# Logits by slots turned out of VectorE's copy behind scores 3, and the max subtraction in two halves by bank

## What is computed

```python
xn = rms_norm(x, gamma_x)
se = rms_norm(slot_embeds, gamma_slot)
logits = jnp.einsum('bsd,etd->bset', xn, se)
dispatch = jax.nn.softmax(logits, axis=1)          # over the tokens s
slots = jnp.einsum('bsd,bset->betd', xn, dispatch)
h = jax.nn.gelu(slots @ w1, approximate=False)
processed = h @ w2
combine = jax.nn.softmax(logits.reshape(b, s, e * t), axis=-1)   # over the slots
out = jnp.einsum('bnd,bsn->bsd', processed.reshape(b, e * t, d), combine)
```

## Time and profile before

| | us |
|---|---|
| median of 3 executions | 509.27 (509.1 to 510.19) |
| the profiled execution | 508.64 |
| its span, first to last instruction | 506.6 |
| TensorE busy, matmuls | 462.0 (91%) |
| VectorE busy | 376.6 (74%) |
| ScalarE busy | 312.4 (62%) |
| GpSimd busy | 175.0 (35%) |

### The profile page before, as it was taken

One profiled execution on the slowest core, in us unless ns is written; L12 is line 12 of the kernel. 1 busy time (PEld: TensorE's weight loads), 2 busy tenths in 40 slices (PEclk: granted clock), 3 DMA queues, 4 the chain that ended last, 5 costly groups with the idle time before them and its releaser, 6 DMA issues.

```text
span 506.6 us, 16039 instructions
## 1 busy us (share of the span) xinstructions
PE 462.0 (91%) x5768; PEld 377.2 (74%) x5768; DVE 376.6 (74%) x937; ACT 312.4 (62%) x544; POOL 175.0 (35%) x278
## 2 busy tenths in 40 slices
PE   3067999999999999999999999999999999999996
PEld 2046787878778787877878787787878778787875
DVE  3878696878868687887968777796877789595651
ACT  3345757566674856667575766757476675747571
POOL 4415143341515234251523425151442425144120
PEclk9559999999999999999999999999999999999999
DMA  2500203030020202011020202002020200202000
GB/s 65 122 6 9 48 12 54 5 56 8 20 45 10 52 9 53 0 30 32 10 52 10 52 0 48 14 10 52 10 52 0 56 6 10 43 12 43 12 3 10
DMA packets 45779, 14.46 MB, mean 29 GB/s; under 512 B 35640, under 2 KB 45624, under 8 KB 45752
## 3 DMA queue, kind: packets, MB, share of 16 engines
q1 hardware_dynamic: 45000, 13.80, 13.3%
q10 hardware_dynamic: 752, 0.30, 0.3%
HBM read 3.61 MB, written 2.10 MB: 11 GB/s over the span
## 4 chain that ended last, share of the span: by engine, by line
PE 74%; DVE 17%; issue 6%; ACTq 1%; ACT 1%; DVEq 0%; POOL 0%; POOLq 0%
PE x L904 14%; PE p_s L942 14%; PE x L1056 13%; PE p_s L960 9%; PE x L1029 6%; PE x L1067 6%; PE p_f L929 3%; DVE maxima L723 3%; DVE maxima L729 3%; PE x L983 2%; PE x L1037 2%; DVE arg L691 2%; PE x L1013 2%; DVE small L675 2%; DVE s_sb L697 2%
## 5 line engine op out<-in xcount | busy, mean ns | idle before, releaser
L436 POOL TENSOR_TENSOR s_sb<-s_sb,causal 128x256 f32<-128x256 f32 x128 | 94.1, 735 | 267.9 <-ACT s_sb L497 267.9
L697 DVE TENSOR_TENSOR s_sb<-p_s,causal 128x384 f32<-128x384 f32 x128 | 70.9, 554 | 62.1 <-PE p_s L942 59.7
L497 ACT ACTIVATE s_sb<-p_s 128x384 f32<-128x384 f32 x128 | 62.7, 490 | 77.2 <-PE p_s L942 77.1
L942 PEld LDWEIGHTS p_s<-feat 64*64 64x64 f32 x2048 | 78.6, 133 | 38.3 <-issue 30.2
L942 PE MATMUL p_s<-feat 64*64 64x256 f32 (+3 forms) x2048 | 100.2, 311 | 5.9 <-DVE s_sb L697 5.0
L492 ACT ACTIVATE feat<-arg,f_bias 128x512 f32<-128x512 f32 x128 | 89.7, 714 | 0.1
L691 DVE TENSOR_SCALAR arg<-p_f,f_low,f_high 128x512 f32<-128x512 f32 x64 | 51.6, 806 | 30.6 <-PE p_f L929 30.6
L1056 PE MATMUL x<-w_sb,hid_t 128*128 128x128 f32 x512 | 65.7, 281 | 0.0
L1056 PEld LDWEIGHTS x<-w_sb,hid_t 128*128 128x128 f32 x512 | 59.6, 191 | 6.6 <-issue 6.6
L960 PE MATMUL p_s<-s_sb,vw 128*32 128x128 f32 x1536 | 48.6, 274 | 5.1 <-DVE s_sb L697 5.1
L691 DVE TENSOR_SCALAR arg<-p_g,f_low,f_high 128x512 f32<-128x512 f32 x64 | 51.4, 802 | 0.0
(11 more groups left out here) (132 smaller groups left out, 835.2 us busy)
## 6 DMA issues: line engine op xcount, KB each, us to landing
xin<-in_L_attn_x_dram SPq DMA_DIRECT2D x32, 64.0 KB, 2.4
out_dram<-out_sb SPq DMA_DIRECT2D x32, 64.0 KB, 2.1
se_rows<-n_L_ffn_slot_embeds_dram SPq DMA_DIRECT2D x1, 256.0 KB, 4.5
w_f<-in_L_ffn_w_dram SPq DMA_DIRECT2D x1, 256.0 KB, 4.6
w_sb<-in_L_ffn_w_dram SPq DMA_DIRECT2D x1, 256.0 KB, 4.5
stack_t<-stack SPq DMA_TRANSPOSE x16, 4.4
bqkv_bc<-in_L_attn_bqkv_dram ACTq DMA_DIRECT2D x1, 192.0 KB, 5.0
wqkv_f<-in_L_attn_Wqkv_dram SPq DMA_DIRECT2D x1, 192.0 KB, 4.9
```

The costliest lines, as they stand in the source:

```text
L436: pool.tensor_tensor(v, v, m, ALU.mult).then_inc(mb_ok, 1)
L497: nc.scalar.activation(s_sb[:, p, 1, :], p_s[:, 1, 0:384], ACT.Copy).then_inc(eb_ok, 1)
L697: nc.vector.tensor_tensor(s_sb[:, p, 0, :], p_s[:, 0, 0:384], causal[:, :], ALU.mult).then_inc(ea_ok, 1)
L942: mm = nc.tensor.matmul(p_s[rows:rows + 64, u, o:o + hi - lo], f[:, T + keys:T + keys + 64], f[:, lo:hi], start=True, stop=True, skip_grou ...
```

## The change

The logits by slots are no longer computed by matmuls from the inputs. VectorE copies each tile of the logits by tokens out of its bank of `x01` into a new buffer `log_sb` in SBUF, and the same instruction gives the maximum of each row as its accumulator output. TensorE then transposes the eight 128 by 128 blocks of `log_sb` into `x23`.

In order: the copies with the token maxima move from stage 3 to stage 2, behind `add_attention` and ahead of `qk_norms`. The transposes stand behind scores 3, ahead of `project(b, 3)`, where the products stood ahead of scores 3. The slot maxima stay ahead of `evac_a(b, 3)`, and each half raises `mx_ok` for itself. `shift` is done in two calls, one for each half of the slots.

```diff
             def token_maxima(b):
 
-                after(dve, lg_ok, count(b, 3, 1))
-                nc.vector.tensor_reduce(maxima[:, 4:6], x01[:, :, :], AX_X, ALU.max)
+                after(dve, lt_ok, count(b, 2, 0))
+                for j in range(TILES):
+                    after(dve, lg_ok, count(b, 2, j + 1))
+                    nc.vector.tensor_scalar(log_sb[:, j, :], x01[:, j, :], 1.0, LOWEST, ALU.mult, ALU.max,
+                                            accum_out=maxima[:, 4 + j:5 + j]).then_inc(lc_ok, 1)
 
             def slot_maxima(b):
 
                 for h in range(2):
-                    after(dve, lg_ok, count(b, 3, 2 + h))
-                    last = nc.vector.tensor_reduce(maxima[:, 2 * h:2 * h + 2],
-                                                   x23[:, h, :].rearrange("p (c t) -> p c t", t=T), AX_X, ALU.max)
-                last.then_inc(mx_ok, 1)
+                    after(dve, lt_ok, count(b, 2, h + 1))
+                    nc.vector.tensor_reduce(maxima[:, 2 * h:2 * h + 2], x23[:, h, :].rearrange("p (c t) -> p c t", t=T),
+                                            AX_X, ALU.max).then_inc(mx_ok, 1)
...
-                    mm = three(x01[:, j, :], hi[:, sl], lo[:, sl], se_hi[:, :], se_lo[:, :], True, False)
-                mm.then_inc(lg_ok, 1)
-
-            def logits_slots(b):
-                hi, lo = xt_hi[:, b[1], :], xt_lo[:, b[1], :]
+                    three(x01[:, j, :], hi[:, sl], lo[:, sl], se_hi[:, :], se_lo[:, :], True, False).then_inc(lg_ok, 1)
+
+            def logits_turned(b):
+                after(pe, lc_ok, count(b, 2, 2))
                 for c in range(NCH):
                     if c % 2 == 0:
                         after(pe, (o1_ok, o2_ok)[c // 2], count(b, 1, 0))
-                    sl = slice(128 * c, 128 * c + 128)
-                    mm = three(x23[:, c // 2, T * (c % 2):T * (c % 2) + T], se_hi[:, sl], se_lo[:, sl], hi, lo,
-                               c % 2 == 0, False)
+                    for j in range(TILES):
+                        o = T * (c % 2) + 128 * j
+                        mm = nc.tensor.matmul(x23[:, c // 2, o:o + 128], log_sb[:, j, 128 * c:128 * c + 128],
+                                              ident[:, :], start=(j == 0 and c % 2 == 0), stop=False,
+                                              is_transpose=True, skip_group_check=True)
                     if c % 2 == 1:
-                        mm.then_inc(lg_ok, 1)
+                        mm.then_inc(lt_ok, 1)
...
-            def shift(b):
-
-                after(pe, mx_ok, count(b, 1, 1))
-                for c in range(NCH):
+            def shift(b, h):
+
+                after(pe, mx_ok, count(b, 2, h + 1))
+                for c in (2 * h, 2 * h + 1):
...
-                mm.then_inc(shd_ok, 1)
+                if h == 1:
+                    mm.then_inc(shd_ok, 1)
```

More of the change, by code:

```diff
@@ L28 @@
 CLIP = 20.0
+LOWEST = -3.0e38
 BLOCKS = ((0, 0, 0, T, 0), (64, 64, 64, T, 64), (128, 0, 128, 192, 256), (192, 64, 128, T, 256))
@@ L159, in build @@
         maxima = sb("maxima", [128, 6], BF16)
+        log_sb = sb("log_sb", [128, TILES, SLOTS])
         disp = sb("disp", [128, TILES, SLOTS])
@@ L251, in build @@
         lg_ok = sem("lg_ok")
+        lc_ok = sem("lc_ok")
+        lt_ok = sem("lt_ok")
         mx_ok = sem("mx_ok")
@@ L850, in row @@
                     if s == 3:
-                        token_maxima(b)
                         slot_maxima(b)
@@ L872, in row @@
                             add_attention(bp)
+                        token_maxima(b)
                         if nxt:
@@ L1015, in shift @@
                                               start=False, stop=True, skip_group_check=True)
-                mm.then_inc(shd_ok, 1)
+                if h == 1:
+                    mm.then_inc(shd_ok, 1)
                 ni = neg_ident[:, :].rearrange("p (a t) -> p a t", a=1).broadcast_to([128, 2, 128])
                 for j in range(TILES):
-                    for h in range(2):
-                        v = x23[:, h, :].rearrange("p (c t) -> p c t", c=2)[:, :, 128 * j:128 * j + 128]
-                        mm = nc.tensor.matmul(v, maxima[:, 4 + j:5 + j].broadcast_to([128, 128]), ni,
-                                              start=False, stop=True, skip_group_check=True)
-                mm.then_inc(shc_ok, 1)
+                    v = x23[:, h, :].rearrange("p (c t) -> p c t", c=2)[:, :, 128 * j:128 * j + 128]
+                    mm = nc.tensor.matmul(v, maxima[:, 4 + j:5 + j].broadcast_to([128, 128]), ni,
+                                          start=False, stop=True, skip_group_check=True)
+                if h == 1:
+                    mm.then_inc(shc_ok, 1)
             def slot_sums(b, half):
@@ L1122, in row @@
                         logits_tokens(b, nxt)
-                        logits_slots(b)
                     if s == 3:
+                        logits_turned(b)
                         project(b, 3)
-                        shift(b)
+                        shift(b, 0)
+                        shift(b, 1)
                     if s == 4:
```

## The result

The changed kernel takes 505.38 us (median of 9, 505.04 to 507.78) against 509.27 in the same comparison (median of 9): a ratio of 0.9927, 95% interval 0.9913 to 0.9941. It is 3.9 us faster, where I had forecast 7.3 us slower. Its profiled execution took 505.23, 3.4 us less than the one before.

A forecast was written before the change was run, and what follows sets the result against it. The VectorE, GpSimd, ScalarE chain was taken to bound out_sb to context, TensorE the rest. Slot maxima 0.51 us later in 14 passes (7.1), plus 0.2 for first and last, gave 516.6 us; range 512.5 to 520.5.

The forecast's parts named there:

- What bounds the kernel: From out_sb to context one chain, VectorE, GpSimd, ScalarE, with TensorE slack 0.33 us; from context on TensorE carries the pass.
- The third stretch: From context to the next out_sb: 19.85 us, TensorE busy for 19.52 of it.
- The wait for the logits and the copies: Behind out_sb on VectorE: 0.94 us waiting until the second copy starts, then that copy, 0.62 plus 0.08 for its accumulator.
- My upper bound: Dearest copy, 0.73 us plus 0.19 accumulator: slot maxima end 0.73 us later, kernel time 519.9 us.
- T: End of VectorE's slot maxima, 3.84 us behind out_sb before; forecast 0.51 later, at 4.35.
- The norms take 1.10 as before: VectorE's qk_norms, now behind the copies and ahead of the slot maxima, were to keep their 1.10 us.
- From T to `context` it takes 5.55 us: Way from the slot maxima's end through qk_newton, GpSimd and ScalarE to context: unchanged at 5.55 us.
- a longer idle time of TensorE ahead of `context`: Sign expected in the new profile: TensorE idle ahead of context for longer than the 0.33 us before.
- C: Rival: hidden room in the chain, as in qk_newton, takes up half the delay; 512 to 513.5 us; chance 0.13.
- A: Rival: TensorE's saved 0.5 us a pass counts, 501.3 us; smaller gain through sooner evac_b(b, 4), 505 to 508; together 0.07.
- The two halves of `shift`: Only the second half stays behind the slot maxima; slot_sums 0.23 us sooner, but the time doesn't change by it.
- TensorE's relief: Twelve products (1.52 us) out, eight transposes (1.00) in: 0.5 us less a pass, ahead of context, only widening a wait.

The follow-up runs named there:

- b_mask: Kernel before, with GpSimd's mask_b(b, 3) moved behind stack_low instead of ahead of qk_apply; 513.40 us against 509.27.
- b_both: Kernel before, with GpSimd's mask_b(b, 3) behind stack_low and residual and place_v behind the pass's last mask; 513.29 us.
- a_whole: Changed kernel with the max subtraction (shift) in one piece again, behind both slot maxima; 517.81 us.
- b_order: Kernel before, with only the token maximum, still a reduction of both tiles, moved ahead of qk_norms; logits by slots stay products; 524.85 us.
- b_late: Kernel before, with GpSimd's residual and place_v for the next sequence behind the pass's last mask instead of behind mask_b(b, 2); 507.19 us.
- b_mask_held: Kernel before, with GpSimd's mask_b(b, 3) behind stack_low, and stack_low made to wait for VectorE's copy stack_again; 505.70 us.
- a_whole_held: Changed kernel with the max subtraction in one piece, and GpSimd's stack_low made to wait for VectorE's copy stack_again; 506.93 us.
- b_halves: Kernel before, with only the max subtraction (shift) split in two halves by bank; 509.86 us.
- a_held_twice: Changed kernel with GpSimd's stack_low waiting for VectorE's stack_again, and project(b, 3)'s matmuls issued twice in each pass; 505.21 us.

## Why the prediction was wrong

*What bounds the kernel.* Right: the chain `out_sb`, VectorE, GpSimd, ScalarE, `context`, and TensorE from there on. The third stretch stayed at 19.84 to 19.98 in the middle passes of all variants. The way from ScalarE's end to `context` stayed at 0.10 where the copy was short; in b_mask, b_both, a_whole and b_order, where it was long, it was 0.70 to 0.88, and the transposes of the slots came last.

*The wait for the logits and the copies.* Right to 0.01: the second copy starts 1.28 behind `out_sb`. The copy's step is 0.61 to 0.62; its accumulator row lasts 0.085 and costs 0.06 behind the first copy and nothing behind the second, where I had put 0.08. So the norms start 0.09 sooner than in the sum. My upper bound had a slip that played no part: a first copy of 0.92 would have held up the second, as it has only 0.69 before that, so T would have been later by 0.96 and not 0.73.

*"The norms take 1.10 as before."* Wrong: 0.84. In the 1.10 there were 0.27 of waiting for GpSimd's residual, and the change moved the norms away from it. Of the 0.33 by which T comes sooner than forecast, this is most. b_late gets the same step back by moving the residual instead.

*"From T to `context` it takes 5.55 us", by a chain that "isn't touched".* This is the step that failed and turned the sign: 5.18, 0.37 to 0.45 less. Here too a stretch that I took over as a duration contained a wait, and what it waited for wasn't behind T but beside it: GpSimd's mask, which hangs on `evac_b(b, 3)` and not on T. So T could move by 0.18 at no cost, and since the mask ended 0.19 sooner behind `out_sb`, `context` came 0.19 sooner. I had placed `evac_b(b, 3)` behind ScalarE's logarithm and exponential, at 278.4, which is 3.59 behind `out_sb`, and asked of the mask only whether it would be done before `qk_n`. It came at 3.29, because the norms ended sooner than in my sum. An estimate from these rows: with it at 3.59 the mask would have ended at 4.94 and the first step of `qk_newton` at 5.02 instead of 4.91, a loss of 0.11 a pass and not of 0.51. b_mask_held shows what the mask held back: with it gone, `stack` comes 0.47 to 0.55 sooner behind T, and the rest of the way is TensorE's 5.23. With 0.51 expected, -0.33 on the first stretch and -0.37 on the second leave about -0.20 a pass. Of my signs, a longer idle time of TensorE ahead of `context` didn't come either: 0.19 instead of 0.33.

*The rivals.* C named the right place, "`qk_newton`, whose first step lasts 0.68 ... seems to hold a wait", and let it take back half of the 0.51; it had no price worked out, and the norms' step, 0.47 for 64 columns, had the same mark. A's time (505 to 508 for a part of it) fits the result by luck. Its mechanism was `evac_b(b, 4)` coming sooner by the halves; but `stack` behind it waited 0.51 for `qk_n`, and what came sooner was `evac_b(b, 3)`. My range ended above the result, as C's share was cut off at half of the shift.

*The two halves of `shift`.* "The time doesn't change by it" was right of the chain and wrong of the kernel: a_whole costs 12.4 us. I had walked the way to `context` on the engines' queues, and had the slack of TensorE right (5.23 against 5.18, as a_whole_held shows), but not the order of two engines at one memory. It is also where the transposes earn something: only with them does the first half start ahead of T, so that the halves bring the copy forward (3.31 behind T); in b_halves they don't (3.58 to 3.66).

*TensorE's relief.* Its 0.23 in a_held_twice was worth nothing, as forecast. But that the products no longer stand ahead of scores 3 is what let `evac_b(b, 3)` come sooner, by the rows; here I had looked at how much work was removed and not at what stood behind it.

## What to carry to other kernels

Before a duration is carried over into a sum, hold it against the same instruction elsewhere and against its size: 0.47 or 0.68 us for 64 columns is a wait, and if its end follows the end of an instruction on the other engine by a constant, it goes or comes as the two move against each other. Then measure the chain through that other instruction too. Where VectorE and GpSimd both work from SBUF, read them side by side, and let a semaphore decide who is first instead of 0.2 us of luck: one wait was worth 8 to 11 us here where the luck had turned. Moving the second engine's work out of the way (b_mask_held) gave as much as rebuilding the first one's.

## What the runs showed that I had not expected

- Some of VectorE's instructions from SBUF to SBUF end a fixed time behind the GpSimd instruction that was running when they began: the norms' step 0.05 to 0.06 behind it (0.47 instead of 0.20), the first step of `qk_newton` 0.08 (0.68 instead of 0.21), and the copy of 512 f16 columns 0.15 (1.13 instead of 0.28). Copies and clips from PSUM, and reductions, kept their length beside GpSimd's work, and so did the reciprocal of `den`, from SBUF to SBUF (0.35).
- A copy of 512 columns from PSUM with its maximum as accumulator output takes as long as the maximum alone (0.690 against 0.686 us), and its second row nearly nothing (all 32 of the changed kernel: busy us, mean ns):

```profile
L729 DVE TENSOR_SCALAR_CACHE_REDUCE log_sb<-x 128x512 f32<-128x512 f32 x32 | 21.3, 690 | 4.3 <-PE x L910 4.3
...
L729 DVE DVE_READ_ACCUMULATOR log_sb<-x 128x1 bf16 x32 | 2.7, 85 | 0.0
```

- Eight transposes of 128 by 128 in fp32 take 1.09 us together. With 0.28 for one alone, the step from one to the next is 0.12.
